# Dense expert layers: the next node group's first layer moved between a group's second layer and its rows, loops written out

## Time and profile before

| what | value |
|---|---|
| median of 3 runs | 11198.45 us |
| the profiled execution's own time | 11192.64 us |
| its span in the profile | 11190.6 us |
| mean granted TensorE clock | 0.788 of full |
| PE busy | 6613.8 us (59%) |
| DVE busy | 4907.6 us (44%) |
| POOL busy | 4446.7 us (40%) |
| ACT busy | 2129.1 us (19%) |

### The profile page before, as it was taken

The page is one execution under the profiler, slowest core; times in us unless marked ns, Lnnn a source line. Parts: engine busy times, 40 slices in busy tenths (PEclk is TensorE's granted clock), DMA queues, the critical chain, the costliest instruction groups (busy, mean ns, idle before and its releaser), DMA issues. The chain is left out here.

```text
span 11190.6 us, 100099 instructions
## 1 busy us (share of the span) xinstructions
PE 6613.8 (59%) x28182; PEld 4970.1 (44%) x28182; DVE 4907.6 (44%) x13525; ACT 2129.1 (19%) x5700; POOL 4446.7 (40%) x4412
## 2 busy tenths in 40 slices
PE   0001228999966755556655555439566777774487
PEld 0000017888844433334433333328535666663355
DVE  7561137888844422223322222541225666665322
ACT  0000004444431200001200000122122333332222
POOL 0647735666600166662046665020205555550000
PEclk9997559999988877776767776659766777776699
DMA  0001003333300333331023332019502222220000
GB/s 12 6 13 16 4 8 105 82 83 83 83 15 8 108 93 93 93 93 40 10 69 94 92 94 77 0 24 312 193 19 71 71 71 72 71 69 6 10 11 17
DMA packets 404399, 696.90 MB, mean 62 GB/s; under 512 B 154143, under 2 KB 267784, under 8 KB 403421
## 3 DMA queue, kind: packets, MB, share of 16 engines
q0 software_dynamic: 206848, 480.68, 15.9%
q1 hardware_dynamic: 197076, 210.68, 5.9%
HBM read 631.46 MB, written 59.47 MB: 62 GB/s over the span
## 5 line engine op out<-in xcount | busy, mean ns | idle before, releaser
L647 POOL DMA_INDIRECT att_rows<-el_table,dst_order_row x1520 | 1560.2, 1026 | 1216.4 <-issue 369.5
L631 PE MATMUL sum_sum<-sum_rows,sum_hot 128*125 128x256 f32 x3520 | 1324.6, 541 | 1192.0 <-issue 477.9
L631 PEld LDWEIGHTS sum_sum<-sum_rows,sum_hot 128*125 128x125 f32 x3520 | 898.0, 268 | 1618.9 <-issue 526.3
L595 POOL DMA_INDIRECT sum_rows<-rel_table,src_order_row x880 | 843.6, 959 | 1162.1 <-ACTq L586 755.7
L595 POOL DMA_INDIRECT sum_rows<-el_table,dst_order_row x880 | 843.6, 959 | 967.0 <-ACTq L586 560.2
L550 POOL DMA_INDIRECT dst_order_record<-records,dst_order_row x784 | 813.6, 1038 | 588.1 <-PEq L454 297.1
L608 DVE TENSOR_TENSOR gnn_acc<-gnn_acc,sum_sum 125x256 f32 x440 | 184.4, 419 | 1869.3 <-DMA ffn0e_w<-in_L_ffn_eW_dram 603.0
L1111 PE MATMUL att_sum<-att_rows,att_hot 128*125 128x265 f32 x1280 | 456.4, 516 | 285.7 <-ACT att_rows L1173 169.9
L647 POOL DMA_INDIRECT dst_order_record<-el_table,dst_order_row x240 | 262.5, 1094 | 522.7 <-SPq L946 301.2
L1111 PEld LDWEIGHTS att_sum<-att_rows,att_hot 128*125 128x125 f32 x1280 | 301.4, 247 | 379.5 <-issue 302.8
L789 PE MATMUL att_found<-gnn_to_dst,att_hot_t 125*128 x1760 | 437.8, 392 | 3.9 <-ACT att_hot_t L838 3.1
(11 more groups left out here) (776 smaller groups left out, 13008.8 us busy)
## 6 DMA issues: line engine op xcount, KB each, us to landing
block_w<-in_L_ffn_W_dram SPq DMA_DIRECT2D x112, 512.0 KB, 6.3
block_w<-in_L_ffn_W_dram SPq DMA_DIRECT2D x56, 1024.0 KB, 6.2
att_rows<-el_table,dst_order_row POOLq DMA_INDIRECT x1520
rel_table<-open_st SPq DMA_DIRECT2D x25, 784.0 KB
sum_rows<-rel_table,src_order_row POOLq DMA_INDIRECT x880
sum_rows<-el_table,dst_order_row POOLq DMA_INDIRECT x880
dst_order_record<-records,dst_order_row POOLq DMA_INDIRECT x784
pairs<-zeros SPq DMA_DIRECT2D x1, 7168.0 KB
```

The source lines that it names most:

```text
L595: nc.gpsimd.indirect_dma_start(rows[l][:, g, :], None, table, bass.IndirectOffsetOnAxis(ap=o["row"][:, k:k + 1], axis=0)).then_inc(s[f"row ...
L631: last = nc.tensor.matmul(sums[u % SUMS][:, 0:D], hot[u % HOTS][:, g, :], rows[l][:, g, :], start=(g == 0), stop=(g == G - 1))
L647: nc.gpsimd.indirect_dma_start(rows[l][:, g, 0:width], None, table, bass.IndirectOffsetOnAxis(ap=o["row"][:, k:k + 1], axis=0)).then_inc(s ...
```

## The change

All loops of `build_experts` over experts and groups are written out, so that every instruction has fixed addresses and fixed semaphore values (in layer 1 the number of the chosen expert stays a register). The steps on TensorE get one list, `order`, in which n counts the groups of all experts one behind the other (T in all, 5 for each expert): the first layer of group n+1 stands behind the hidden layers of group n, and the rows of group n come after both. The two PSUM buffers are taken in turn along this list. Where there is one hidden layer only (layer 1), h has two buffers, by groups; otherwise one for each layer, as before. The rows wait for VectorE's first operation on the group before (`rows_used`), no longer for its last. SyncE waits for the rows of the expert two before, no longer for VectorE's addition. The unused argument `affine` goes.

```diff
-        h = [sb(f"h{l}", [part[l], blocks[l], GN]) for l in range(1, L)]
+        h = [[sb(f"h{l}_{n}", [part[l], blocks[l], GN]) for n in range(2 if L == 2 else 1)] for l in range(1, L)]
...
+        order = [(0, 0, g) for g in range(blocks[1])]
+        for n in range(T):
+            order += [(n, l, g) for l in range(1, L - 1) for g in range(blocks[l + 1])]
+            if n + 1 < T:
+                order += [(n + 1, 0, g) for g in range(blocks[1])]
+        at = {job: q for q, job in enumerate(order)}
+        hidden_of = lambda n, l: h[l][n % len(h[l])]
+        last_job = lambda n, l: at[n, l, blocks[l + 1] - 1]
...
             @block.sync
             def _(sp):
                 sp.dma_start(brow[:], last_bias).then_inc(s["loaded"], 16)
-                    if not first:
-                        until(sp, DV, "x", (e - 1) * GROUPS - 1)
...
+                for n in range(experts):
+                    if n >= P:
+                        sp.wait_ge(s["rows"], (n - 1) * GROUPS)
...
             @block.tensor
             def _(pe):
-                def body(e, p, before):
-                    pe.wait_ge(s[f"w_in{p}"], (e - p) * (8 * NL) + 16 * NL)
-                    pe.sem_inc(s["pe_passed"], 1)
-                    with pe.Fori(0, GROUPS) as i:
...
+                def hide(n, l):
+                    e, i = n // GROUPS, n % GROUPS
+                    m_, w = part[l + 1], wt[e % P][l]
+                    if l == 0 and i == 0:
+                        pe.wait_ge(s[f"w_in{e % P}"], 16 * NL * (e // P + 1))
+                    if l:
+                        pe.wait_ge(s["kept"], last_job(n, l - 1) + 1)
+                    src = [XT[:, k, i * GN:(i + 1) * GN] if l == 0 else hidden_of(n, l - 1)[:, k, :] for k in range(blocks[l])]
+                    for g in range(blocks[l + 1]):
+                        q = at[n, l, g]
+                        if q >= 2:
+                            pe.wait_ge(s["kept"], q - 1)
+                        product_t(nc, fb[q % 2], m_, [(w[:, k, g * 128:g * 128 + m_], src[k]) for k in range(blocks[l])]).then_inc(s["hidden"], 1)
+
+                def add_rows(n):
+                    pe.wait_ge(s["kept"], last_job(n, L - 2) + 1)
+                    if n:
+                        pe.wait_ge(s["rows_used"], n)
+                    f, w = hidden_of(n, L - 2), wt[n // GROUPS % P][L - 1]
+                    product_rows(nc, rows, [(f[:, k, :], w[:, k, :]) for k in range(blocks[L - 1])]).then_inc(s["rows"], 1)
+
+                hide(0, 0)
+                for n in range(T):
+                    for l in range(1, L - 1):
+                        hide(n, l)
+                    if n + 1 < T:
+                        hide(n + 1, 0)
+                    add_rows(n)
...
             @block.scalar
             def _(act):
+                for q, (n, l, g) in enumerate(order):
...
+                    act.wait_ge(s["hidden"], q + 1)
+                    nc.scalar.activation(dense(hidden_of(n, l)[:, g, :]), slices(fb[q % 2][0:m_, :]), func, bias=layer_bias[l][0:m_, col],
+                                         scale=layer_scale[l][0:m_, col] if layer_scale else 1.0).then_inc(s["kept"], 1)
...
             @block.vector
             def _(dve):
+                for n in range(T):
...
+                    dve.wait_ge(s["rows"], n + 1)
+                    if n:
+                        dve.wait_ge(s["added"], n)
+                    v.tensor_tensor(t[:], rows, brow[:, bass.ds(which, 1), :].to_broadcast([R, GT, D]), ALU.add).then_inc(s["rows_used"], 1)
+                    dve.wait_ge(s["rows_used"], n + 1)
+                    if gate is not None:
+                        own(v.tensor_tensor(t[:], t[:], col_of(gate[:, e * TILES + i * GT:e * TILES + (i + 1) * GT], D), ALU.mult))
+                    v.tensor_tensor(x, x, t[:], ALU.add).then_inc(s["added"], 1)
```

More of the change, by code:

```diff
@@ L1851, in _, with build_experts @@
                     own.end()
-def build_experts(nc, tag, XT, target, experts, dims, weights, last_bias, gate, func, layer_bias, layer_scale=None, affine=None, chosen=None):
+def build_experts(nc, tag, XT, target, experts, dims, weights, last_bias, gate, func, layer_bias, layer_scale=None, chosen=None):
     L = len(dims) - 1
@@ L1862, in build_experts @@
     P = min(experts, 2)
+    T = experts * GROUPS
     with ExitStack() as ctx:
@@ L1866, in build_experts @@
         wt = [[sb(f"w{l}_{p}", [part[l], blocks[l], dims[l + 1]]) for l in range(L)] for p in range(P)]
-        h = [sb(f"h{l}", [part[l], blocks[l], GN]) for l in range(1, L)]
-        xe = sb("xe", [128, KB, GN]) if affine else None
+        h = [[sb(f"h{l}_{n}", [part[l], blocks[l], GN]) for n in range(2 if L == 2 else 1)] for l in range(1, L)]
         brow, t = sb("brow", [R, 8 if chosen is not None else experts, D]), sb("t", [R, GT, D])
@@ L1871, in build_experts @@
         rows = wide[0:R, 0:GT * D].rearrange("p (j x) -> p j x", j=GT)
-        jobs = [(l, g) for l in range(L - 1) for g in range(blocks[l + 1])]
-        names = [f"h{l}_{g}" for l, g in jobs]
+        order = [(0, 0, g) for g in range(blocks[1])]
[6 more added lines that the diff above has]
+        last_job = lambda n, l: at[n, l, blocks[l + 1] - 1]
         NL = sum(blocks[:L])
[L1875 to L1878, removed]
+        with phase(nc, tag, "loaded", "w_in0", "w_in1", "hidden", "kept", "rows", "rows_used", "added", "chain") as s, nc.Block() as block:
             def number(eng, e):
                 return e if chosen is None else eng.value_load(chosen[0:1, e:e + 1], min_val=0, max_val=7)
[L1884 to L1892, removed]
             @block.sync
@@ L1896, in _ @@
                 sp.dma_start(brow[:], last_bias).then_inc(s["loaded"], 16)
-                def load(e, p, first):
-                    if not first:
-                        until(sp, DV, "x", (e - 1) * GROUPS - 1)
-                        sp.sem_inc(s["sp_passed"], 1)
-                    e = number(sp, e)
+                for n in range(experts):
+                    if n >= P:
+                        sp.wait_ge(s["rows"], (n - 1) * GROUPS)
+                    e = number(sp, n)
                     for l in range(L):
@@ L1904, in load @@
                         for k in range(blocks[l]):
[L1905 to L1911, removed]
+                            sp.dma_start(wt[n % P][l][:, k, :], weights[l][bass.ds(e * dims[l] + k * 128, part[l])]).then_inc(s[f"w_in{n % P}"], 16)
@@ L1937, in _ @@
-                each_expert(pe, body)
+                def hide(n, l):
[11 more added lines that the diff above has]
+                        product_t(nc, fb[q % 2], m_, [(w[:, k, g * 128:g * 128 + m_], src[k]) for k in range(blocks[l])]).then_inc(s["hidden"], 1)
@@ L1939, in _ @@
             @block.scalar
             def _(act):
[L1941 to L1957, removed]
@@ L1958, in _ @@
-                each_expert(act, body)
+                which = {}
+                for q, (n, l, g) in enumerate(order):
+                    if n // GROUPS not in which:
+                        which[n // GROUPS] = number(act, n // GROUPS)
+                    m_, col = part[l + 1], bass.ds(which[n // GROUPS] * blocks[l + 1] + g, 1)
+                    act.wait_ge(s["hidden"], q + 1)
+                    nc.scalar.activation(dense(hidden_of(n, l)[:, g, :]), slices(fb[q % 2][0:m_, :]), func, bias=layer_bias[l][0:m_, col],
+                                         scale=layer_scale[l][0:m_, col] if layer_scale else 1.0).then_inc(s["kept"], 1)
@@ L1962, in _ @@
                 v = nc.vector
+                own = Chain(dve, s["chain"])
                 dve.wait_ge(s["loaded"], 16)
[L1964 to L1980, removed]
+                for n in range(T):
+                    e, i = n // GROUPS, n % GROUPS
+                    if i == 0:
+                        which = number(dve, e)
+                    x = target[:, i * GT:(i + 1) * GT, :]
+                    dve.wait_ge(s["rows"], n + 1)
[6 more added lines that the diff above has]
+                    v.tensor_tensor(x, x, t[:], ALU.add).then_inc(s["added"], 1)
 def put_in(nc, tag, pairs, fill=(), pool_work=None):
```

## The result

The changed kernel takes 10995.08 us in the median of 4 runs (10992.06 to 10995.88); the kernel before, run beside it, 11199.35. The ratio is 0.9817, with a 95% interval of 0.9803 to 0.9832, so the gain is clear of the noise. I had forecast 10996 and a range of 10975 to 11030. The time is hit, but two errors cancel in it, as the phases show.

A forecast was written before the change was run, and what follows sets the result against it. TensorE, stalled each time until ScalarE has kept a layer's last product, bounds four phases; gains of 111.9+66.5+9.7+13.9 = 202.0 us off 11192.64 give 10990.6, forecast 10996 with the run median's 5.8 us offset, range 10975 to 11030.

The forecast's parts named there:

- TensorE's stalls bound the phases: All four phases: TensorE stands still twice a group (once in ffn1e) until ScalarE is done; reordered, no such wait is late.
- The sum for ffn3e: ffn3e's cycle: four products of 2.12 us and rows of 4.21, 12.69 for 15.56, gaining 111.9 us over 39 cycles.
- The sum for ffn0e: ffn0e's cycle: 2.12+1.08+2.35 = 5.55 us for 9.05, gaining 66.5 us over 19 cycles.
- The two new neighbours: On TensorE, product after small product and product after rows: unseen in the trace, between nothing and 0.33 us each, taken at nothing.
- The clock in ffn0e: Rival: TensorE's clock in ffn0e keeps falling because of small shapes; 11010 to 11018 us, chance 0.12. Forecast assumed 2.4 GHz kept.
- The wait that stays late: Rival: one of the two TensorE stalls in each group remains, half the gain is lost, 11097 us; chance 0.04.
- the change does nothing: Rival: something the waits don't show sets the order on TensorE, so the time stays at 11198 us; chance 0.02.
- Fetching the written-out code: Rival: fetching 3410 written-out matmuls, some 25 packets, slows TensorE; slower than before from 8 us a packet; chance 0.02.
- VectorE next: In ffn0e VectorE's three operations, about 5.1 us with waits, become next under the 5.55 us cycle; margin 0.45 us.
- (d): Rows wait for VectorE's first operation on the rows before, 0.23 us to start, 1.49 to run; ffn0e's products cover 3.2.
- ffn1e and ffn0s: ffn1e: stalls 14.4 us, table loads 1.5, less 2.0 lost at the end, net 13.9; ffn0s: 9.7 us gained.
- Writing out costed at nothing: Loop branches on TensorE are already hidden, so writing out gains nothing there; at most 2 us over 75 turns.

The follow-up runs named there:

- x4: The change, with ffn0e's second-layer product using 128 columns of first-layer weights as stationary operand instead of 64: 10432.02 us on another chip, ffn0e cycle 5.73 us for 5.86.
- x6: The change, with both ffn0e's second-layer product and its rows filled to 128-wide operands: 10426.54 us on another chip, ffn0e cycle 5.34 us for 5.86.
- x2: Kernel before written out in its old order, plus two unread matmuls behind each hidden layer in ffn0e: ratio 0.9957 to the kernel before, ffn0e clock 0.98.
- x3: The change, but the rows wait again for VectorE's last operation on the group before, not its first: ratio 0.9841 to the kernel before.
- x9: The change's order, with TensorE and ScalarE in loops with register waits in ffn0e and ffn3e: 11001.05 us, ratio 0.9824 to the kernel before.
- x1: Written out as in the change, but TensorE in the old order: ratio 0.9972 to the kernel before.

## Why the prediction was right, and where it was not

- *TensorE's stalls bound the phases, and the new order covers them.* Right. One wait for ScalarE is left at each end of a phase with two hidden layers, none late in between.
- *The sum for ffn3e.* The mechanism was right, the rows' term mis-sized: I put 4.21 us, measured from weight load to weight load, beside products of 2.12 measured from matmul to matmul. In the changed kernel:

```profile
10602.20 4.18 PEld L1272 LDWEIGHTS ffn3e_wide<-ffn3e_w,ffn3e_h 128*125 128x125 f32 x20
10602.30 4.48 PE L1272 MATMUL ffn3e_wide<-ffn3e_w,ffn3e_h 128*125 128x256 f32 x20
...
10606.62 1.84 PE L1261 MATMUL ffn3e_fb<-ffn3e_h,ffn3e_w 128*128 128x500 f32 x4
...
10608.74 1.84 PE L1261 MATMUL ffn3e_fb<-ffn3e_h,ffn3e_w 128*128 128x500 f32 x4
...
10615.11 4.48 PE L1272 MATMUL ffn3e_wide<-ffn3e_w,ffn3e_h 128*125 128x256 f32 x20
```

  From the first matmul of the rows to the next product's it is 4.32 us (10602.30 to 10606.62). The loads run ahead of their matmuls by different times: by 0.21 us behind the rows (10719.34 and 10719.55, which stood in the earlier trace rows), by 0.10 for the rows' own load in the new order (10602.20 and 10602.30), so from matmul to matmul it is 4.21+0.21-0.10. From rows to rows it is 12.81. The 0.12 us missing, 38 times, is the 4.4 us by which this phase fell short.
- *The sum for ffn0e.* The two new neighbours, which I took at nothing within bounds of 0 to 0.33 us, cost 0.12 in the small product (1.20 us, 3503.55 to 3504.75, for 1.08) and 0.20 in the product behind it (2.32, 3504.75 to 3507.07, for 2.12). The cycle is 0.31 us longer for it, 18 times, 5.6 of the 5.8 us missing. The row of 0.33 us behind 64-feature rows was the nearest, being also a change of size, and I should have taken it (x4 to x6).
- *The clock in ffn0e.* That stalls and not small shapes let it fall is shown by x2 and, from the other side, by x3. The rival with 0.12 is out.
- *The wait that stays late* and *the change does nothing* are out by the waits above.
- *Fetching the written-out code.* In ffn3e the instruction queue moved 16 packets:

```profile
q8 instruction: 16, 0.26, 0.2%
```

  TensorE's idle time of 2 us there is the two waits for ScalarE, so no cost of a packet shows. I had estimated 25 for the four phases.
- *VectorE next.* Its cycle is shorter than I thought: its operations start 1.53 us apart (3503.66, 3505.19, 3506.71), where the two steps of the earlier trace rows took 3.38 us together. That is 4.54 us in all, with 1.32 idle in each group of ffn0e, not under 0.6. The margin is 1.3 us, not 0.45. The edit that lets the rows go ahead of VectorE's last two operations, waiting for `rows_used`, was named as (d) but not priced; x3 prices it at 37 us.
- *ffn1e and ffn0s* came within 0.4 us each: 14.4+1.5-2.0 against 13.5, 9.7 against 9.3. In ffn1e there is luck in it: its cycle is 17.12 us for 17.0, the same 0.12 as in ffn3e and 1.0 us in eight turns, and 0.5 of it came back because the clock rose sooner at the start (3.7 us after the first matmul, for 5.1 before). The one wait for VectorE at its end, costed at 2.0 us, took 1.7.
- *The forecast of the time* is 0.9 us off, which says less than it seems. The phases gave 11.0 us less than forecast; 5.8 us outside of them, and the places of the two profiled executions among their runs, made up for it.
- *Writing out costed at nothing* is right for the new order (x9), and wrong as a statement on the kernel before, where it is worth 19 us in the phases (x1).

## What to carry to other kernels

Where TensorE waits for the engine that empties PSUM, put a step of the next tile between, and check each wait for the time of the work ahead of it; the wait for the slow engine's last operation must be moved to its first one too, or a good part is lost again. A stall of 1 us costs more than itself where it comes often enough to bring the clock down, as it did in ffn0e and not in ffn3e. When adding up steps, measure all of them between the same kind of start, and price a boundary between operands of different sizes by the nearest boundary of that kind, not at nothing.

## What the runs showed that I had not expected

- A change of the stationary operand between full size (128x128 or 128x125), 64x125 and 128x64 costs TensorE 0.13 to 0.20 us at the boundary; the three changes in ffn0e's cycle cost 0.52 on top of 5.34 us.
- In written-out code TensorE resumes 0.12 to 0.19 us earlier after another engine's signal than in the loops (ffn3e's cycle in the old order: 15.56 to 15.26 us).
- The first microseconds of a phase vary by when the clock rises: ffn0s lasted 48.1 us in one execution of the change and 46.7 in another, with the same 30.9 us between its bias additions; the clock rose 6.0 us after the first matmul in the one and 3.7 in the other.
- One transfer that spreads 1000 KB of biases over all partitions ahead of the weights kept TensorE waiting 9 us in each of two phases; behind them it delays nobody. With it the kernel takes 10974 us, 0.18% under the change, the best version that was measured twice.
